# Routing of a fused transformer block: top-k rounds dealt out anew, the root asked for earlier in two batches, base tiles opened together, rank sums ahead of the mask

## The reference, cut to what matters

```python
# block 1: gated mix of the tokens, learned adjacency
sim = einsum('bhnd,bhmd->bnm', Q, K) / (sqrt(d) * H)          # (b, 256, 256), from ctx_512
threshold = top_k(sim, 76)[0][:, :, -1:]
A = sigmoid(sim) * (sim >= threshold)
A = (A + swapaxes(A, -1, -2)) * 0.5
x = x + tanh(g_xattn[0]) * ((1 - gamma) * layernorm(x) + gamma * A)
# block 2: 64 experts, 8 for each token
xn = layernorm(x)
probs = softmax(xn @ gate_w.T)                                 # (1024, 64)
topk_w, topk_idx = top_k(probs, 8)
x = x + tanh(g_ffn[0]) * sum over the 8 experts of topk_w * (silu(g) * u) @ w2_e.T
# blocks 3 and 4: causal attention against ctx_512, and 8 experts plus a shared one
```

## Time and profile before

| | |
|---|---|
| median of 3 runs | 612.97 us (612.03 to 613.97) |
| the profiled execution's own time | 607.06 us |
| its span | 605.3 us |
| TensorE busy | 425.7 us (70%) |
| DVE busy | 346.5 us (57%) |
| ScalarE busy | 184.0 us (30%) |
| POOL busy | 146.3 us (24%) |
| mean granted TensorE clock | 0.834 |

### The profile page before, as it was taken

How to read it: one execution, slowest core, us unless ns; L and a number is a source line. 1 busy time by engine, 2 the same in 40 slices (tenths; PEclk the granted TensorE clock), 3 DMA queues, 4 the chain that set the end, 5 groups by cost and what they waited for, 6 DMA issues and landing times.

```text
span 605.3 us, 9222 instructions
## 1 busy us (share of the span) xinstructions
PE 425.7 (70%) x2738; PEld 355.7 (59%) x2738; DVE 346.5 (57%) x1050; ACT 184.0 (30%) x377; POOL 146.3 (24%) x154
## 2 busy tenths in 40 slices
PE   5065553302999999997136637899699978999686
PEld 3043342202998889885025425787488856887586
DVE  2978875396344444443367803487547883681554
ACT  3212210100333333343611412525252342517231
POOL 1306675673000000002775370001710000000000
PEclk9976565555999999997557756999779996999899
DMA  7996222266699999993332130000310000000000
GB/s 272 427 410 264 88 96 79 78 238 211 209 301 322 324 312 326 377 396 128 100 91 67 38 104 0 1 2 16 100 44 0 2 0 0 18 2 2 2 17 18
DMA packets 36693, 82.96 MB, mean 137 GB/s; under 512 B 6000, under 2 KB 16048, under 8 KB 34864
## 3 DMA queue, kind: packets, MB, share of 16 engines
q1 hardware_dynamic: 22800, 55.83, 26.3%
q0 software_dynamic: 6144, 16.79, 8.6%
q10 hardware_dynamic: 7712, 9.90, 4.6%
HBM read 50.44 MB, written 31.92 MB: 136 GB/s over the span
## 4 chain that ended last, share of the span: by engine, by line
PE 52%; DVE 15%; issue 12%; ACT 7%; POOL 6%; another core or an unknown queue 4%; DMA 2%; SPq 1%; DVEq 0%; POOLq 0%; ACTq 0%
PE PS L555 11%; PE PS L565 7%; POOL slots_in L432 5%; PE PS L644 4%; PE PS L618 4%; PE PS L542 3%; PE PS L764 2%; PE PS L657 2%; PE PS L712 2%; PE PS L659 2%; PE PS L658 2%; DVE TH L1312 2%; DVE WORK L1049 2%; DVE TOP L1045 2%
## 5 line engine op out<-in xcount | busy, mean ns | idle before, releaser
L442 POOL DMA_INDIRECT GB<-slots_out,IDXG x64 | 68.4, 1069 | 214.9 <-SPq L365 139.7
L555 PE MATMUL PS<-XTE,WR 128*128 128x128 f32 (+2 forms) x512 | 79.7, 299 | 0.0
L432 POOL DMA_INDIRECT slots_in<-XNA,IDX x64 | 64.9, 1014 | 36.8 <-issue 27.6
L555 PEld LDWEIGHTS PS<-XTE,WR 128*128 128x128 f32 x512 | 70.2, 193 | 0.6 <-ACT XTE L854 0.4
L1234 DVE TENSOR_TENSOR HE<-SGE,PS 128x128 f32<-128x128 f32 (+2 forms) x64 | 20.0, 312 | 62.9 <-ACT SGE L863 60.0
L565 PE MATMUL PS<-WR,HE 128*80 128x256 f32 (+2 forms) x198 | 53.6, 381 | 0.3 <-DVE HE L1234 0.3
L657 PE MATMUL PS<-XH,WGH 128*128 128x256 f32 x160 | 49.7, 311 | 0.3 <-DVE XL L1430 0.3
L854 ACT COPY XTE<-PS 128x256 f32<-128x256 f32 (+2 forms) x64 | 26.3, 410 | 74.5 <-PE PS L542 70.6
L644 PE MATMUL PS<-WD,XW 128*128 128x256 f32 x160 | 41.8, 384 | 7.0 <-DVE XW L1319 3.5
L542 PE MATMUL PS<-CF,XE 80*128 80x80 f32 (+2 forms) x198 | 28.3, 256 | 25.7 <-DMA XE<-slots_in 25.7
L658 PE MATMUL PS<-XL,WGH 128*128 128x256 f32 x160 | 45.3, 283 | 0.0
(11 more groups left out here) (226 smaller groups left out, 843.2 us busy)
## 6 DMA issues: line engine op xcount, KB each, us to landing
WR<-in_wexp SPq DMA_DIRECT2D x64, 384.0 KB, 5.0
slots_in<-GB SPq DMA_DIRECT2D x12, 1024.0 KB, 18.7
XE<-slots_in SPq DMA_DIRECT2D x24, 160.0 KB, 4.5
slots_out<-OE ACTq DMA_DIRECT2D x24, 160.0 KB, 4.3
XE<-slots_in SPq DMA_DIRECT2D x29, 128.0 KB, 5.2
slots_out<-OE ACTq DMA_DIRECT2D x29, 128.0 KB, 5.1
WGU<-in_wgu SPq DMA_DIRECT2D x1, 2560.0 KB
XE<-slots_in SPq DMA_DIRECT2D x11, 192.0 KB, 4.0
```

The costliest lines, as they stand in the source:

```text
L432: pool.indirect_dma_start(out=xs, out_offset=bass.IndirectOffsetOnAxis(ap=IDX[:, t, j:j + 1], axis=0), in_=XNA[:, t, :], in_offset=None, b ...
L442: pool.indirect_dma_start(out=GB[:, t % BT, j, :], out_offset=None, in_=ys, in_offset=bass.IndirectOffsetOnAxis(ap=IDXG[:, t, j:j + 1], ax ...
L555: last = mm(psGE[place % 2][:, a, 0:cap(place)], W13[:, k, a, :], XTE[:, place % 2, k, 0:cap(place)], start=(k == 0), stop=(k == KC - 1))
```

## The change

Four edits, all in routing. The number of rounds, scatters, roots and matmuls stays the same.

1. The rounds of the next batch are dealt out by a list of bounds. Batch 0: 2, 1, 2, 0 and 5 rounds (ahead of stats, norm, choose, place, and behind place) where it was 2, 1, 2, 1 and 4. Batches 1 and 2: 3, 2, 3, 1 and 1.
2. The root of batch 1 stays behind the 10th scatter of batch 0. Those of batches 2 and 3 stand behind the 7th scatter of the batch ahead of them.
3. `mix` writes both base tiles ahead of the wait for `masked`, and marks the start of accumulation once for the bank.
4. `ranks` sums the tiles of earlier batches ahead of the wait for `mask_ready`. Behind it 3 matmuls are left in every batch.

```diff
@@ -57,7 +57,10 @@
 NORM_STEPS = 2 * BT + 2 + 3 * NEWTON
 LOWEST = -3.0e38
 
-POW_AT = 2
+ROOT_BEHIND = (None, 10, 7, 7)
+
+FIRST_ROUNDS = (2, 3, 5, 5)
+LATER_ROUNDS = (3, 5, 8, 9)
 SIM_SCALE = 1.0 / 16.0
 HEAD_SCALE = HD ** -0.5
 
@@ -427,8 +430,9 @@
                 pool.wait_ge(S["xn_ready"], t // BT + 1)
                 pool.wait_ge(S["idx_ready"], t // BT + 1)
                 for j in range(TOP0):
-                    if t % BT == BT - 1 and j == POW_AT and t // BT + 1 < B:
-                        norm_scale(t // BT + 1)
+                    b = t // BT + 1
+                    if b < B and t % BT * TOP0 + j == ROOT_BEHIND[b]:
+                        norm_scale(b)
                     pool.indirect_dma_start(out=xs, out_offset=bass.IndirectOffsetOnAxis(ap=IDX[:, t, j:j + 1], axis=0),
                                             in_=XNA[:, t, :], in_offset=None, bounds_check=SLOTS - 1, oob_is_err=False)\
                         .then_inc(S["scattered"], 16)
@@ -477,12 +481,12 @@
                 pe.wait_ge(S["base_ready"], b + 1)
                 pe.wait_ge(S["x1_kept"], b)
                 for t in range(BT):
-                    mm(psT[:, t, :], ident, BASES[b % 2][:, t, :], start=True, stop=False)
-                    if t == 0:
-                        pe.wait_ge(S["masked"], b + 1)
+                    mm(psT[:, t, :], ident, BASES[b % 2][:, t, :], start=(t == 0), stop=False)
+                pe.wait_ge(S["masked"], b + 1)
+                for t in range(BT):
                     mm(psT[:, t, :], ident, AM[:, t, :], start=False, stop=False)
                     for c in range(BT):
-                        last = mm(psT[:, t, c * P:(c + 1) * P], AM[:, c, t * P:(t + 1) * P], ident, start=False, stop=(c == BT - 1))
+                        last = mm(psT[:, t, c * P:(c + 1) * P], AM[:, c, t * P:(t + 1) * P], ident, start=False, stop=(t == BT - 1 and c == BT - 1))
                 last.then_inc(S["summed"], 1)
 
             def logits(b):
@@ -502,13 +506,16 @@
                 last.then_inc(S["logits_done"], 1)
 
             def ranks(b):
+                first = b * BT
+                pe.wait_ge(S["idx_ready"], b)
+                for t in range(BT):
+                    for m in range(first):
+                        mm(psR[:, t, :], onesb, MB[:, m, :], start=(t == 0 and m == 0), stop=False)
                 pe.wait_ge(S["mask_ready"], b + 1)
-                pe.wait_ge(S["idx_ready"], b)
-                for t in range(BT):
-                    n = b * BT + t
-                    for m in range(n):
-                        mm(psR[:, t, :], onesb, MB[:, m, :], start=(m == 0), stop=False)
-                    last = mm(psR[:, t, :], before, MB[:, n, :], start=(n == 0), stop=True)
+                for t in range(BT):
+                    for m in range(first, first + t):
+                        mm(psR[:, t, :], onesb, MB[:, m, :], start=False, stop=False)
+                    last = mm(psR[:, t, :], before, MB[:, first + t, :], start=(b == 0 and t == 0), stop=(t == BT - 1))
                 last.then_inc(S["ranked"], 1)
 
             scores(0)
@@ -1135,21 +1142,22 @@
             for b in range(B):
                 mask(b)
                 ahead = b + 1 < B
+                to_stats, to_norm, to_choose, to_place = FIRST_ROUNDS if b == 0 else LATER_ROUNDS
                 if ahead:
                     dve.wait_ge(S["sim_copied"], b + 2)
-                    top_rounds(b + 1, 0, 2)
+                    top_rounds(b + 1, 0, to_stats)
                 mix_stats(b)
                 if ahead:
-                    top_rounds(b + 1, 2, 3)
+                    top_rounds(b + 1, to_stats, to_norm)
                 mix_norm(b)
                 if ahead:
-                    top_rounds(b + 1, 3, 5)
+                    top_rounds(b + 1, to_norm, to_choose)
                 choose(b)
                 if ahead:
-                    top_rounds(b + 1, 5, 6)
+                    top_rounds(b + 1, to_choose, to_place)
                 place(b)
                 if ahead:
-                    top_rounds(b + 1, 6, ROUNDS)
+                    top_rounds(b + 1, to_place, ROUNDS)
             st.end()
 
             st = Steps(dve, S["dve_w8"])
```

More of the change, by code:

```diff
@@ L504, in ranks @@
             def ranks(b):
-                pe.wait_ge(S["mask_ready"], b + 1)
+                first = b * BT
                 pe.wait_ge(S["idx_ready"], b)
                 for t in range(BT):
-                    n = b * BT + t
-                    for m in range(n):
-                        mm(psR[:, t, :], onesb, MB[:, m, :], start=(m == 0), stop=False)
-                    last = mm(psR[:, t, :], before, MB[:, n, :], start=(n == 0), stop=True)
+                    for m in range(first):
+                        mm(psR[:, t, :], onesb, MB[:, m, :], start=(t == 0 and m == 0), stop=False)
+                pe.wait_ge(S["mask_ready"], b + 1)
+                for t in range(BT):
+                    for m in range(first, first + t):
+                        mm(psR[:, t, :], onesb, MB[:, m, :], start=False, stop=False)
+                    last = mm(psR[:, t, :], before, MB[:, first + t, :], start=(b == 0 and t == 0), stop=(t == BT - 1))
                 last.then_inc(S["ranked"], 1)
```

## The result

The changed kernel took 625.01 us (median of 4 runs, 620.58 to 625.51), the kernel before beside it 612.50 (median of 4, 609.38 to 613.97): 1.0195 times the time before, 95% interval 1.0133 to 1.0257. It is slower, by 12.5 us, where 606.0 was forecast. The profiled execution took 624.63 with a span of 622.8.

A forecast was written before the change was run, and what follows sets the result against it. No engine was taken as full; POOL's scatters, waiting for `IDX` at batch heads, set the experts' start. The sum for the last scatter, -7.0 us, took 612.97 to 606.0; range of 8 in 10: 603.8 to 610.8.

The forecast's parts named there:

- part 6: Rank sums ahead of the mask: no cost; if keys still came 3.4 us behind choose, batch 2 starts 1.4 us later.
- rival three: Gain given back behind 147 us, by an unlucky clock or a transfer gating the experts: 608 to 611; 7 in 100.
- parts 4 and 5: Scatters of batches 2 and 3 start at 91.5 (-4.1 us) and 113.0 (-7.5), with POOL binding.
- Parts 1 to 5 and 7: Base tiles ahead of the mask (-0.85 us per batch, or 0), the four batches' scatter starts, and the last 16 scatters.
- part 7: Last 16 scatters all run beside DVE's weights: +0.5 us, bounds 0 and +1.
- part 2: Batch 0: base tiles and earlier keys sum to -1.7 us, first scatter at 45.7.
- parts 3 and 4: Scatters of batch 1 start at 70.0 (-0.7 us), those of batch 2 at 91.5 (-4.1).
- Part 5: Batch 3: POOL comes 3.3 us behind its data; first scatter at 113.0 instead of 120.46, -7.5 us.
- Part 8: TensorE's clock at the experts: taken as 0, worth at most 1.7 us either way.
- The first: Late signals ahead of the keys belong to the profiled execution only; timed gain 2.9 us, 610.1; 25 in 100.
- The second: Late signal is real and follows the last matmul whatever is moved: +1.4 us, 607.4 to 608.4; 12 in 100.
- The slower rival: Scatters of batches 1 to 3 slow down when nothing separates them; 618 us with 0.25 more each; 3 in 100.

The follow-up runs named there:

- after_again: The changed kernel, unchanged, run again beside the kernel before: 586.05 us, ratio 0.9982.
- after_pool_waits: The changed kernel with one more wait: POOL begins the last batch's scatters only when the experts' count is signalled; 582.98 us, ratio 0.9954 to the kernel before.
- after_pool_waits_2: The changed kernel with POOL waiting for the count ahead of the last batch's scatters, second run: 581.35 us, ratio 0.9940 to the kernel before.
- after_old_rounds: The changed kernel with the rounds dealt out as before: 622.67 us in one run, beside 613.11 for the kernel before.
- bursts_flood: A separate kernel, nothing of the model: bursts of matmuls read by DVE beside POOL's scatters, plus 96 small transfers; 149.73 us where the kernel before took 613.11.
- after_old_roots: The changed kernel with the roots of batches 2 and 3 behind the 10th scatter again: 612.33 us in one run, beside 613.11 for the kernel before.
- after_pool_waits_4: The changed kernel with POOL waiting for the count ahead of the last batch's scatters, fourth run: 612.62 us, ratio 1.0012 to the kernel before.
- after_count_held: The changed kernel with the 16 counting matmuls kept back until POOL is in its last batch: 625.72 us, ratio 1.0177 to the kernel before.

## Why the prediction was wrong

**The step that failed is part 6, with the sentence on the weights under rival three.** Part 6 read the 1.93 and 3.23 us ahead of the keys as the size of a late signal, bounded it at 3.4 us behind choose, and found it covered. It was not a size. The signals came 1.7 and 1.6 us after POOL had stopped, wherever that was. The pause made the wait short, and parts 4 and 5 of my own sum remove the pause. Rows for this stood in front of me: both late signals fell within POOL's waits for `IDX`, at nearly the same distance from the stop. (That they fell into the waits says nothing alone, since `IDX` needs the keys.) And the row that spoke for short bursts, batch 0 with its 3 matmuls signalled at once, stands at 45.13, ahead of the first scatter at 47.40: it could not tell few matmuls from a POOL that issues nothing. And "weights of the experts are asked for earlier too, so I see no gate" priced the count by its matmuls' records. It is the signal that has all weights and slots of the experts behind it, and it was held 20.6 us. The sum of what follows: `counted` at 134.45, `ORD` at 138.02, weights in SP's queue to 149.6, slots 10.26 us later, 160.1. The experts start 13.1 us later, where the medians have 12.5: this is the slowdown.

**Parts 1 to 5 and 7 were right where signals are prompt.** In `after_again` the batches begin at 45.64, 69.85, 91.35 and 112.86, and the root of batch 2 is a dead heat at 78.51. In part 7, I put the last 16 scatters at 15.6 + 2.6 = 18.2 us. Their row in `after_again` (us, POOL busy, granted clock, DMA share, GB/s):

```profile
112.90:136.20 23.30, 18.22 (x16) 0.50 0.63 225
```

The Trainium skill ("GPSIMD Engine Reference", 8, Key points) has GpSimd contend with VectorE's two-input instructions for the SBUF interfaces; the two runs agree with it, 18.22 us beside the weights and 15.52 in the changed kernel of the result, where DVE stood still until 134.45.

In the call of the result itself, part 2 held (45.77), and parts 3 and 4 missed by 2.4 and 5.3 us, each by a held signal ahead of `MB` or the keys. Part 5's gapless POOL came true (0.30 ahead of 118.26), and with it the harm.

**Part 8** took 0 for the clock behind the experts. TensorE worked the first 4.5 us of them at a granted clock of 0.50 in both traces (147.0 to 151.5 and 160.0 to 164.5), and 3.9 of the 4.4 us above lie beside the gathers.

**The rivals.** The first asked whether the late signals belong to the profiled execution alone. They don't: a holding call takes 25 us more in its timed runs too, and a prompt call has no late signal in its profiled ones. (Every timed run comes with a span and a granted clock, so each was recorded in some form, and no run here was taken without. That recording itself holds the signals in some calls is not excluded.) And what the prediction held against it, "nothing else in the trace is that late", was misread: in the same trace ScalarE waits 3.58, 6.29 and 4.88 us on "remote" from 345.7 to 363.6 (the rows above). But its arithmetic is, by luck, what prompt calls show: the kernel before starts its batches there 2.0 and 4.2 us earlier (forecast 1.9 and 4.1), and the gain at the experts is 2.4 us (forecast 2.9). In the medians it is 1.2 us, and 4.3 and 5.2 with the wait of `after_pool_waits` added; of all these ratios only that of `after_pool_waits_2` excludes 1. The second had the cause, a real late signal, and the wrong law for it: +1.4 us instead of +19. The slower rival named the wrong mechanism; the scatters never slowed down by more than part 7 has. What was missing is one that couples the two: a POOL without pauses, which I took for the gain, holds back the signals that everything behind depends on.

## What to carry to other kernels

A wait that ends on "remote", with no work in the records before it, has a releaser all the same: lay it beside the other engines in order of time and ask what they did at that moment, before a size is written down for it. Before a gap of one engine is closed, list the signals of the others that arrive in it. And one count that has the order of all later loads behind it should be asked for early or given a pause of its own: one wait on POOL cost nothing in the prompt calls, and in the holding one the ratio to the kernel before was 1.0012, where the changed kernel without it had 1.0195.

## What the runs showed of the hardware

**Signals are held while GpSimd issues indirect transfers without a pause, in some calls.** The count's matmuls, ended by their records, were read 14.2 to 20.6 us later by DVE in the three kernels without a pause ahead of batch 3, and a burst up to 38.8 us later in `bursts_flood`. Where POOL stopped, the signal came 1.1 to 1.9 us later in eleven cases: in `before` (91.84 to 93.56, 116.83 to 118.39), in the changed kernel (67.26 to 68.73, 93.63 to 94.73), in `after_old_roots` (93.76 to 95.57, 118.84 to 120.59), in `after_pool_waits_4` (67.27 to 68.81, 118.08 to 119.64) and in `after_count_held` (67.23 to 68.73, 93.64 to 95.57, 139.22 to 140.33). ScalarE's came 2.7 us later (101.06 to 103.74). A hold also ends while POOL goes on issuing (134.45 and 129.06 for the count), and what ends it then is not known. It is not only TensorE's signals to DVE: DVE's wait ahead of 68.73 in the changed kernel is for its own previous instruction, done at 66.5, and ScalarE's reads at 349.30 to 363.64 are beside gathers instead of scatters. One case stands apart: the burst read at 122.54 in `bursts_flood`, 9.4 us behind the end of the last scatter.

**The condition belongs to the call, not to the kernel or the chip.** The kernel before took 587.3, 587.29, 586.58 and 587.9 us in four calls and 612.5, 613.11 and 611.98 in three; one chip gave 587.3 in one call and 613.11 in another. Records go missing with it. Of the 1025 increments of `scattered`, the trace has all in each of the nine profiles of the model's kernels from prompt calls, and 421, 292, 209, 394, 333 and 291 in the holding ones (before, after, `after_old_rounds`, `after_old_roots`, `after_pool_waits_4`, `after_count_held`).

The Trainium skill ("NOTIFIC — the notification-queue block", 7.1, Overflow) says that this block's inner pipeline always holds back the producers rather than lose a record inside it, and could throttle an engine so; records are dropped, by the same section, in one of its modes where the ring behind it is full. Held signals and missing records fit the two, but no run here shows the block.

**Left open.** What makes a call a holding one is not known, nor whether there would be one without recording. Whether a single counting matmul would be signalled in time was therefore only measured where all signals are prompt. The 96 small transfers were in the one burst kernel that met a holding call; whether the scatters alone would have held its signals was not measured.
